# The first expert pair of each pass moved from steps 1 to 3 to steps 3 to 5, with four kept output tiles

## The chip, the core and the metric

The kernel runs on one core of a Trainium2 chip. The core has four compute engines that work side by side: TensorE (PE in the rows), VectorE (DVE), ScalarE (ACT) and GpSimd (POOL). SyncE (SP) issues DMAs and computes nothing here; POOL issues the indirect ones. The metric is the device time of one execution in microseconds. Three timed runs of the kernel before gave 3048.73, 3056.23 and 3058.16 us; the median is 3056.23 us.

## The reference, cut to what matters

32 images of 32 x 32 tokens with 128 channels pass through three layers, each added to its input:

```
x = x + shifted_window_attention(groupnorm(x))     # 8 heads of 16, windows of 64 tokens, scaled cosine
t = t + banded_attention(layernorm(t))             # 4 heads of 32, windows of 128, the last 33 keys
t = t + experts(layernorm(t))                      # below
probs = softmax(xf @ gate_w + gate_b)
top2_vals, top2_idx = top_k(probs, 2)              # each token goes to 2 of 8 experts
h = gelu(xf @ w1[e] + b1[e])                       # 128 -> 256
y = h @ w2[e] + b2[e]                              # 256 -> 128
out = sum over the two experts of share * y
```

The reference computes every expert for every token. The kernel computes only the two chosen ones: tokens are scattered to a buffer in DRAM that is sorted by expert, and read back in tiles of 512 slots that belong to one expert each.

## The kernel before, in words

The program is a pipeline over images. A pass `i` (-1 to 34) works on image `i` in the first attention, on `i - 1` and `i - 2` in the second, on `i - 3` in the gate, and on expert tiles of image `i - 4` or older. Each pass has 8 steps `t` of one kind: every engine walks through the same list of steps, and semaphores keep them together. A step holds the softmax of one 128-token tile of either attention (names that end in `_a` and `_b`) and some pieces of the other stages. The order on each engine is written out by hand and no scheduler changes it.

The chain of one step is: PE makes scores (L625, L635) in `bank_s`; DVE adds the bias (L1500, L1503) and takes row maxima (L1508); POOL subtracts the maxima (L1133); ACT takes the exponential (L984); PE transposes (L686); ACT copies (L979); PE multiplies by the values in the next step (L695 to L708). The start of L1500 is the start of a step in what follows.

The expert work is 135 tiles of 512 slots. One image's scattered tokens are a batch: four tiles, made into two pairs (the first batch has one tile, the last one 18). A pass has two slots, 0 and 1, for one pair each. A pair goes through three stages in three steps:

- `into`: PE transposes the tokens of the pair into `bank_m` (`slots_in`, L743) and ACT copies them to `xe` (L1005) and the rows' numbers to `back_to` (L1008).
- `mid`: PE multiplies by the first weights (`hidden`, L752), ACT applies gelu (L1015). ACT loads the table of gelu ahead of it (L1109) and the table of exp behind it (L1036).
- `back`: PE multiplies by the second weights (`expert_out`, L759), DVE adds the bias (L1485) and multiplies by the share into `yo` (L1491).

Slot 0 has its stages in steps 1, 2, 3; slot 1 in steps 6, 7 and step 0 of the next pass. Both use the one PSUM pair `bank_m`, one after the other. SP loads each tile's tokens and weights (`load_pair`, L457 and L459) into one of 4 buffers. POOL adds `yo` to the output in DRAM with an indirect accumulating DMA of 128 rows (`add_back`, L1157), four to a tile; the first of the four waits until the tile before has landed. `BACK_AT` says in which step, counted from the pair's own pass, each of a pair's eight add-backs stands: 8 is step 0 of the next pass. POOL also scatters a new image's tokens, 16 indirect DMAs a pass (L1140), four each in steps 5, 6, 7 and 0.

`plan()` deals pairs to slots: slot 0 takes a pair from pass `batch + 5` on, slot 1 from pass `batch + 4` on. What is left after pass 33 is the tail: pairs that run one after the other in four sets of PSUM banks, with nothing beside them but the add-backs.

## Time and profile before

| what | value |
|---|---|
| median of 3 runs | 3056.23 us |
| the profiled execution: its own time | 3051.38 us |
| the profiled execution: span | 3049.6 us |
| mean granted TensorE clock | 0.891 |
| PE, DVE, ACT, POOL busy | 79%, 66%, 59%, 62% of the span |
| PE in slices 2 to 34 of 40 | 0.8 or 0.9 busy |
| POOL at the end | alone; it ends the span |

The trace covers one execution. Its span is 1.8 us shorter than the time of that execution, and that time is 4.85 us under the median. The busy shares are means over three different stretches: filling (to about pass 6), the full pipeline (passes 7 to 31), and the tail. No engine is full in any of them by its mean; the length is set step by step.

### The profile page before, as it was taken

How to read it: one execution, taken by the hardware profiler on the slowest of the kernel's cores; microseconds unless marked ns; L12 is line 12 of the kernel's file. 1: busy time of each engine (PE TensorE's matmuls, PEld its weight loads, DVE VectorE, ACT ScalarE, POOL GpSimd, SP SyncE). 2: the span in 40 equal slices, each digit the busy share in tenths (PEclk: the TensorE clock that was granted, in tenths of full speed). 3: DMA queues.
4: the chain of work that ended last, by engine and by line, in shares of the span. 5: the costliest groups of instructions: out<-in, count | busy, mean ns of one | idle time of the engine just before them, and what ended most of it. 6: DMA issues, size and time to landing. Idle time of an engine off the chain costs nothing. (4 is left out here: it accounts for less than half of the span.)

```text
span 3049.6 us, 72894 instructions
## 1 busy us (share of the span) xinstructions
PE 2417.9 (79%) x26418; PEld 1716.6 (56%) x26418; DVE 1998.0 (66%) x5670; ACT 1786.3 (59%) x3430; POOL 1897.7 (62%) x1569
## 2 busy tenths in 40 slices
PE   6898888888888888888888888888888888765650
PEld 3465556566556666565556666565566666553440
DVE  3588876777677777776776776777776777662110
ACT  3666666666666666666666666666666666542220
POOL 0224455766666666766666667766666667776666
PEclk8999989999999999989999999999999999877775
DMA  2011122333333333323333333333333323335442
GB/s 77 16 34 37 48 71 55 81 67 70 71 74 74 77 76 63 81 62 74 70 74 74 77 65 76 80 63 75 70 74 74 77 56 71 82 62 141 89 82 26
DMA packets 247793, 210.77 MB, mean 69 GB/s; under 512 B 35260, under 2 KB 204360, under 8 KB 247248
## 3 DMA queue, kind: packets, MB, share of 16 engines
q0 software_dynamic: 94144, 69.54, 16.1%
q1 hardware_dynamic: 153296, 136.58, 15.9%
q8 instruction: 215, 3.52, 0.5%
q14 instruction: 138, 1.13, 0.1%
HBM read 119.73 MB, written 90.77 MB: 69 GB/s over the span
## 5 line engine op out<-in xcount | busy, mean ns | idle before, releaser
L1157 POOL DMA_INDIRECT out_dram<-yo,back_to x540 | 855.3, 1584 | 228.2 <-issue 174.4
L1133 POOL TENSOR_TENSOR s_sb_a<-s_sb_a,mx_a 128x512 f32<-128x512 f32 x256 | 282.4, 1103 | 771.1 <-DVE mx_a L1508 770.8
L1140 POOL DMA_INDIRECT x_sorted<-xn_c,place_i x512 | 515.3, 1006 | 138.9 <-issue 133.4
L1500 DVE TENSOR_TENSOR s_sb_a<-bank_s,bias_a 128x512 f32<-128x512 f32 x256 | 176.0, 687 | 308.4 <-PE bank_s L625 251.4
L1133 POOL TENSOR_TENSOR s_sb_b<-s_sb_b,mx_b 128x512 f32<-128x512 f32 x256 | 289.2, 1130 | 6.9 <-DVE mx_b L1508 6.9
L759 PE MATMUL bank_m<-wk_e,hid 128*128 128x128 f32 x1840 | 282.0, 327 | 0.9 <-ACT hid L1015 0.9
L759 PEld LDWEIGHTS bank_m<-wk_e,hid 128*128 128x128 f32 x1840 | 279.9, 244 | 1.7 <-issue 1.7
L752 PE MATMUL bank_m<-xe,wk_e 128*128 128x512 f32 x460 | 231.4, 628 | 34.4 <-ACT hid L1015 25.8
L686 PE MATMUL bank_to<-k_consts,p_sb_b 128*128 128x128 f32 x1024 | 182.7, 305 | 88.1 <-ACT pt_sb_a L979 76.7
L984 ACT ACTIVATE p_sb_a<-s_sb_a 128x512 f32<-128x512 f32 x256 | 160.5, 627 | 149.8 <-POOL s_sb_a L1133 149.8
L979 ACT ACTIVATE pt_sb_b<-bank_to 128x512 f32<-128x512 f32 x256 | 152.6, 596 | 155.4 <-PE bank_to L686 154.8
L625 PE MATMUL bank_s<-kk_a,q_a 32*64 32x128 f32 x4096 | 123.3, 295 | 129.0 <-ACT sq_a L949 43.2
L1015 ACT ACTIVATE hid<-bank_m,wk_e 128x512 f32<-128x512 f32 x230 | 154.0, 686 | 66.8 <-PE bank_m L752 60.3
L686 PEld LDWEIGHTS bank_to<-k_consts,p_sb_b 128*128 128x128 f32 x1024 | 116.4, 150 | 134.3 <-ACT pt_sb_a L979 118.8
L686 PE MATMUL bank_to<-k_consts,p_sb_a 128*128 128x128 f32 x1024 | 169.3, 289 | 26.2 <-ACT p_sb_a L984 22.0
L984 ACT ACTIVATE p_sb_b<-s_sb_b 128x512 f32<-128x512 f32 x256 | 161.4, 630 | 44.4 <-POOL s_sb_b L1133 42.2
L1485 DVE TENSOR_TENSOR bank_m<-bank_m,wk_e 128x512 f32<-128x512 f32 x115 | 80.2, 699 | 149.5 <-PE bank_m L759 149.5
L1503 DVE TENSOR_TENSOR s_sb_b<-bank_s,k_consts 128x512 f32<-128x512 f32 x256 | 174.2, 680 | 5.5 <-PE bank_s L635 5.5
L1508 DVE TENSOR_REDUCE mx_a<-s_sb_a 128x8 f32<-128x512 f32 x256 | 173.0, 676 | 0.4
L1508 DVE TENSOR_REDUCE mx_b<-s_sb_b 128x4 f32<-128x512 f32 x256 | 173.0, 676 | 0.4
L996 ACT ACTIVATE sum_inv<-bank_to 128x256 f32<-128x256 f32 (+1 forms) x268 | 99.9, 373 | 124.0 <-PE bank_to L708 104.8
L625 PEld LDWEIGHTS bank_s<-kk_a,q_a 32*64 32x64 f32 x4096 | 65.1, 131 | 178.9 <-issue 177.3
(230 smaller groups left out, 5761.9 us busy)
## 6 DMA issues: line engine op xcount, KB each, us to landing
wk_e<-in_w_experts_dram SPq DMA_DIRECT2D x127, 321.0 KB, 3.3
xs<-x_sorted SPq DMA_DIRECT2D x127, 260.0 KB, 2.8
xin<-in_x_dram SPq DMA_DIRECT2D x128, 112.0 KB
x_res<-in_x_dram SPq DMA_DIRECT2D x256, 56.0 KB
out_dram<-t SPq DMA_DIRECT2D x256, 56.0 KB
out_dram<-yo,back_to POOLq DMA_INDIRECT x540, 3.4
x_sorted<-xn_c,place_i POOLq DMA_INDIRECT x512
x_res<-in_x_dram SPq DMA_DIRECT2D x256, 8.0 KB
```

Source lines behind the costliest of these rows:

```text
L625: last = mm(S[r][WTOK * j:WTOK * j + WTOK, 0:P].rearrange("p (h n) -> p h n", h=2), q_flat[rows, window(2 * ta + j)], keys[rows, :, window ...
L686: last = tr(T[:, P * j:P * j + P], p_sb[w][:, j, :], ident)
L752: mm(banks[:, ch, :], w[:, P * ch:P * ch + P], xe[:, m, :], start=True, stop=True).then_inc(z_ready, 1)
L759: last = mm(banks[:, m, P * j:P * j + P], hid[:, CH * m + ch, P * j:P * j + P], w[:, HID + P * ch:HID + P * ch + P], start=(ch == 0), stop ...
L984: func(flat(p_sb[w][:, :, :]), flat(s_sb[w][:, :, :]), ACT.Exp, scale=1.0 if w == 0 else float(DB) ** -0.5).then_inc(p_ready[w], 1)
L1015: func(hid[:, CH * m + ch, :], banks[:, ch, :], ACT.Gelu, bias=w[:, B1_AT + ch:B1_AT + ch + 1]).then_inc(gelu_ready, 1)
L1133: pool.tensor_tensor(s[:, :, :], s[:, :, :], m[:, :, None].to_broadcast(shape), ALU.subtract).then_inc(s_sub[w], 1)
L1140: pool.indirect_dma_start(out=x_sorted.ap(), out_offset=bass.IndirectOffsetOnAxis(ap=place_i[:, d % 2, TILES * choice + t:TILES * choice + ...
L1157: pool.indirect_dma_start(out=out, out_offset=bass.IndirectOffsetOnAxis(ap=back_to[:, q % IDS, j:j + 1], axis=0), in_=yo[:, q % YO, j, :], ...
L1500: tt(s_sb[0][:, :, :].rearrange("p (r h) n -> p r (h n)", h=2), scores, bias_a[:, kind, :, :].rearrange("p (r h) n -> p r (h n)", h=2), AL ...
L1503: tt(s_sb[1][:, :, :], scores, const("mask_b")[:, None, :].to_broadcast([P, HB, P]), ALU.add).then_inc(s_added[1], 1)
L1508: dve.tensor_reduce(mx_s[w][:], s_sb[w][:, :, :], AX_X, ALU.max).then_inc(s_max[w], 1)
```

## The change

Slot 0 moves from steps 1, 2, 3 to steps 3, 4, 5. It now takes a pair from pass `batch + 4` on, as slot 1 does, so that both slots of a pass work on the two pairs of one batch. SP loads both pairs together, where it loaded slot 1's alone; the load of the next pass's slot 0, later in the pass, is gone. `yo` holds 4 tiles in place of 3. The add-backs of slot 0 stand in steps 6, 7, 8, 9 (one each) and 10 (four), those of slot 1 in 11 and 12 (four each).

```diff
-IDS, YO = 8, 3
+IDS, YO = 8, 4
-BACK_AT = ((4, 4, 4, 4, 5, 6, 7, 8), (9, 9, 9, 9, 10, 10, 10, 10))
+BACK_AT = ((6, 7, 8, 9, 10, 10, 10, 10), (11, 11, 11, 11, 12, 12, 12, 12))
@@ plan()
-            if i >= pairs[u].batch + (5 if n == 0 else 4) and i < PASSES - FREE_PASSES:
+            if i >= pairs[u].batch + 4 and i < PASSES - FREE_PASSES:
@@ stage()
-            into = slot(i, 0) if t == 1 else slot(i, 1) if t == 6 else None
-            mid = slot(i, 0) if t == 2 else slot(i, 1) if t == 7 else None
-            back = slot(i, 0) if t == 3 else slot(i - 1, 1) if t == 0 else None
+            into = slot(i, 0) if t == 3 else slot(i, 1) if t == 6 else None
+            mid = slot(i, 0) if t == 4 else slot(i, 1) if t == 7 else None
+            back = slot(i, 0) if t == 5 else slot(i - 1, 1) if t == 0 else None
@@ sync
-                if here[1] is not None:
-                    load_pair(sp, here[1])
+                for u in here:
+                    if u is not None:
+                        load_pair(sp, u)
                 if on(a):
                     load_residual(a, 0)
-                following = slots[i + 1][0] if i + 1 < PASSES else None
-                if following is not None:
-                    load_pair(sp, following)
@@ tensor, step
-                if t == 1:
+                if t == 3:
                     read_slots()
@@ scalar, step
-                if t == 1 and into is not None:
+                if t == 3 and into is not None:
                     slots_copy(into, bank_m)
```

On PE, from the score matmuls of step 4 (L625) to the first matmul of the gate's places and the q and k projections, the kernel before has:

```order
L759 MATMUL bank_m<-wk_e,hid 128x128 x16
L658 MATMUL bank_s<-wqkv_s,xt_b 128x128 x4
...
L686 MATMUL bank_to<-k_consts,p_sb_a 128x128 x4
L625 MATMUL bank_s<-kk_a,q_a 64x128 x8
L635 MATMUL bank_s<-k_b,q_b 128x128 x4
L686 MATMUL bank_to<-k_consts,p_sb_b 128x128 x4
L670 MATMUL bank_to<-chosen,earlier 128x72
```

The same place of the changed kernel, whose lines are two lower (L757 is `expert_out`, L750 `hidden`, L741 `slots_in`):

```order
L741 MATMUL bank_m<-k_consts,xs 128x128 x8
L684 MATMUL bank_to<-k_consts,p_sb_a 128x128 x4
L623 MATMUL bank_s<-kk_a,q_a 64x128 x8
L633 MATMUL bank_s<-k_b,q_b 128x128 x4
L684 MATMUL bank_to<-k_consts,p_sb_b 128x128 x4
L750 MATMUL bank_m<-xe,wk_e 128x512 x4
L668 MATMUL bank_to<-chosen,earlier 128x72
```

The 16 matmuls of `expert_out` have left step 3, the transposes of `slots_in` have come to its end, and the 4 of `hidden` stand between the transposes of step 4 and the matmul L670 (now L668).

On POOL, from the subtraction of step 1 to the one of step 5, the kernel before has (L1133 is the subtraction, L1157 the add-back, L1140 the scatter):

```order
L1133 TENSOR_TENSOR s_sb_b<-s_sb_b,mx_b 128x512
L1157 DMA out_0_dram<-yo,back_to 33280x128 x4
L1133 TENSOR_TENSOR s_sb_a<-s_sb_a,mx_a 128x512
L1133 TENSOR_TENSOR s_sb_b<-s_sb_b,mx_b 128x512
L1157 DMA out_0_dram<-yo,back_to 33280x128 x4
L1133 TENSOR_TENSOR s_sb_a<-s_sb_a,mx_a 128x512
L1133 TENSOR_TENSOR s_sb_b<-s_sb_b,mx_b 128x512
L1133 TENSOR_TENSOR s_sb_a<-s_sb_a,mx_a 128x512
L1133 TENSOR_TENSOR s_sb_b<-s_sb_b,mx_b 128x512
L1157 DMA out_0_dram<-yo,back_to 33280x128 x4
```

The changed kernel (L1131 the subtraction, L1155 the add-back):

```order
L1131 TENSOR_TENSOR s_sb_b<-s_sb_b,mx_b 128x512
L1155 DMA out_0_dram<-yo,back_to 33280x128
L1131 TENSOR_TENSOR s_sb_a<-s_sb_a,mx_a 128x512
L1131 TENSOR_TENSOR s_sb_b<-s_sb_b,mx_b 128x512
L1155 DMA out_0_dram<-yo,back_to 33280x128 x4
L1131 TENSOR_TENSOR s_sb_a<-s_sb_a,mx_a 128x512
L1131 TENSOR_TENSOR s_sb_b<-s_sb_b,mx_b 128x512
L1155 DMA out_0_dram<-yo,back_to 33280x128 x4
L1131 TENSOR_TENSOR s_sb_a<-s_sb_a,mx_a 128x512
L1131 TENSOR_TENSOR s_sb_b<-s_sb_b,mx_b 128x512
L1155 DMA out_0_dram<-yo,back_to 33280x128 x4
```

Before, steps 1, 2 and 4 have four add-backs and step 3 none. Now step 1 has one, and steps 2, 3 and 4 have four each. At the end of POOL's program the tail has 88 add-backs in place of 96.

## Rows read from the trace of the kernel before

**Rows 1.** Busy time by stretch: start:end, length, engines (instructions), TensorE clock, DMA share, GB/s

```profile
413.00:488.10 75.10, 62.77 (x753) 44.69 (x753) 56.63 (x170) 49.38 (x98) 40.05 (x37) 0.89 0.28 74
488.10:576.60 88.50, 75.05 (x817) 53.86 (x817) 61.80 (x177) 55.75 (x107) 56.08 (x47) 0.88 0.31 69
576.60:2549.70 1973.10, 1656.19 (x18791) 1192.78 (x18791) 1417.25 (x4049) 1277.73 (x2439) 1330.50 (x1105) 0.92 0.34 72
2549.70:2810.00 260.30, 184.58 (x1649) 135.07 (x1649) 148.02 (x434) 115.31 (x225) 187.34 (x155) 0.82 0.40 86
2810.00:3049.60 239.60, 97.55 (x464) 73.90 (x464) 26.75 (x41) 36.46 (x63) 149.24 (x96) 0.69 0.43 72
```

**Rows 2.** The same view, pass 19: its steps 0 to 7 in order

```profile
1522.08:1532.24 10.16, 8.94 (x124) 8.03 (x124) 8.55 (x24) 5.53 (x12) 8.41 (x8) 1.00 0.41 102
1532.24:1542.77 10.53, 9.45 (x113) 7.87 (x114) 8.17 (x29) 4.02 (x10) 8.25 (x7) 0.84 0.40 57
1542.77:1554.76 11.99, 9.42 (x90) 5.04 (x89) 6.06 (x18) 10.87 (x23) 9.18 (x7) 0.98 0.61 127
1554.76:1568.52 13.76, 12.09 (x128) 11.24 (x129) 9.59 (x20) 5.00 (x12) 2.03 (x2) 0.77 0.06 10
1568.52:1579.56 11.04, 8.20 (x90) 4.24 (x88) 8.17 (x41) 5.29 (x9) 8.02 (x6) 0.85 0.59 146
1579.56:1588.70 9.14, 6.81 (x81) 3.64 (x81) 4.82 (x11) 8.24 (x13) 6.33 (x7) 1.00 0.16 29
1588.70:1596.39 7.69, 6.54 (x101) 5.51 (x101) 7.61 (x21) 6.55 (x14) 6.56 (x6) 1.00 0.25 48
1596.39:1607.45 11.06, 10.11 (x97) 6.00 (x97) 8.03 (x16) 10.03 (x20) 9.06 (x10) 1.00 0.28 60
```

**Rows 3.** The same view, pass 6: its steps 1 to 3

```profile
422.97:432.58 9.61, 8.49 (x104) 6.91 (x105) 8.17 (x28) 3.62 (x9) 6.84 (x5) 0.82 0.30 50
432.62:439.41 6.79, 5.42 (x82) 3.51 (x80) 6.65 (x18) 5.25 (x15) 3.59 (x3) 1.00 0.81 203
439.41:447.35 7.94, 6.13 (x96) 5.07 (x97) 7.80 (x17) 4.89 (x11) 2.49 (x2) 1.00 0.04 12
```

**Rows 4.** Order of time, PE: start, duration, instruction, count, idle time before and its releaser

```profile
1546.18 1.96 PE L752 MATMUL bank_m<-xe,wk_e 128*128 128x512 f32 x4 [0.79 <-ACT hid L1015]
1556.34 5.98 PE L759 MATMUL bank_m<-wk_e,hid 128*128 128x128 f32 x32
...
1571.64 0.22 PE L670 MATMUL bank_to<-chosen,earlier 128*128 128x72 bf16 x1 [2.78 <-DVE ot_b L1524]
1571.97 3.31 PE L726 MATMUL bank_s<-xn_a,wq_s 128*128 128x512 f32 x4
1575.12 1.88 PE L726 MATMUL bank_s<-xn_a,wk_s 128*128 128x512 f32 x4
...
1587.67 0.48 PE L625 MATMUL bank_s<-kk_a,q_a 32*64 32x128 f32 x16 [1.44 <-ACT sq_a L949]
...
1589.16 1.04 PE L743 MATMUL bank_m<-k_consts,xs 128*128 128x128 f32 x8
...
2698.86 3.74 PE L759 MATMUL bank_m<-wk_e,hid 128*128 128x128 f32 x32
```

**Rows 5.** Order of time, POOL, pass 19 and the tail

```profile
1530.11 0.97 POOL L1140 DMA_INDIRECT x_sorted<-xn_c,place_i  x1 [0.30 <-issue]
...
1538.34 1.57 POOL L1157 DMA_INDIRECT out_dram<-yo,back_to  x1 [0.30 <-issue]
...
3007.36 1.55 POOL L1157 DMA_INDIRECT out_dram<-yo,back_to  x1 [2.46 <-DVE yo L1491]
```

**Rows 6.** Order of time, ACT, the stage mid of pass 19

```profile
1547.37 1.49 ACT L1015 ACTIVATE hid<-bank_m,wk_e 128x512 f32<-128x512 f32 x2 [0.76 <-PE bank_m L752]
1548.88 1.28 ACT L1036 ACT_TABLE_LOAD   x1
```

**Rows 7.** DMA issues on SP, slot 1's first tile of pass 19

```profile
1543.69 0.38 SPq L457 DMA_DIRECT2D xs<-x_sorted  x1
```

## The prediction

> **What bounds the kernel now.** I read the busy time by long stretches first. Passes 8 to 30 are 23 passes in 1973.10 us, 85.8 us each, so that stretch is 65% of the span; pass 6, in which only slot 1 is filled, took 75.10 and pass 7, the first with both, 88.50. Passes 31 to 34 take 260.3 us up to the tail, and the tail 239.6 [rows 1]. The reader is to see that a change to a pass counts some 24 times, and one to the tail once.
>
> Then the same view by steps, pass 19 [rows 2]. No engine fills its step. The longest steps are those of slot 0: step 2 (11.99 us, ACT busy 10.87) and step 3 (13.76 us, PE busy 12.09, TensorE clock 0.77 of full, POOL busy 2.03). Steps 5 and 6 have no second or third stage of a pair and take 9.14 and 7.69. In pass 6, which has slot 1 but not slot 0, steps 1 to 3 take 9.61, 6.79 and 7.94, and there DVE is the full engine (6.65 of 6.79, 7.80 of 7.94) [rows 3]. So slot 0 costs 0.92 + 5.20 + 5.82 = 11.9 us where it stands now. Third, the timeline of PE: in step 3 the 32 matmul records of `expert_out` take 5.98 us at the low clock, 3.74 at the full one; in step 4 PE stands idle 2.78 us until DVE has written `ot_b`, and the q projection behind takes 3.31 where the like k projection takes 1.88; in step 5 it waits 1.44 for ACT's `sq_a` [rows 4]. Those idle times are where the three stages go.
>
> **The change, part by part.** I take a pass as pass 19 and work out its steps anew.
>
> Steps 1 and 2 lose slot 0. I give them pass 6's 9.61 and 6.79 [rows 3].
>
> Step 3 gains the transposes of `into`, 1.04 us on PE [rows 4], between the value products and the transposes of the probabilities. Step 3 is then DVE's, 7.94 us, and DVE gets nothing. The delay reaches the next step's scores by a few tenths: 8.3.
>
> Step 4 gains `hidden` of two tiles, 1.96 + 0.79 + 1.96 = 4.7 us with the wait for gelu between [rows 4]. It stands ahead of L670, which waits 2.78 us anyhow, so 1.9 show. PE is busy in that gap, and the q projection may run at the full clock, 1.88 for 3.31: -1.4. ACT gets two table loads of 1.28 us [rows 6] and four gelus; it is busy 5.29 of 11.04 [rows 2], and its `xe` copy at the end of step 3 decides when `hidden` starts. That start depends on POOL, below. Without it: 11.04 + 1.9 - 1.4 = 11.5, and 0.2 to 0.4 for the copy, 11.8. If the clock falls all the same, 13.2.
>
> Step 5 gains `expert_out`, 3.74 us at the full clock [rows 4]. It stands ahead of the norms' matmuls, whose results ACT waits for. PE has 9.14 - 6.81 = 2.3 us free [rows 2], of which 1.44 is the wait for ACT that would have ended anyhow. I take 2.0 to show: 11.1. Bounds: 1.4 (all free time used) and 3.7 (none). DVE's four operations here find it 4.82 of 9.14 busy.
>
> Steps 6, 7 and 0 stay: 7.69, 11.06, 10.16 [rows 2]. Sum so far: 10.16 + 9.61 + 6.79 + 8.3 + 11.8 + 11.1 + 7.69 + 11.06 = 76.5 us.
>
> POOL then has to be laid over this. An add-back is 1.57 + 0.30 = 1.87 us, a scatter 1.27, the two subtractions of a step 2.03 and some 0.16 [rows 2, 5]. A pass has 16 of each DMA and eight pairs of subtractions: 29.9 + 20.3 + 17.5 = 68 us. That fits in 76.5, but not step by step: with four add-backs steps 2, 3 and 4 need 9.7 us each, 29.0 in all, against 6.8 + 8.3 + 11.8 = 26.9. POOL may start 1.9 us into step 2 (L1500 to the maxima), is free 11.5 us in, and the maxima of step 3 are there at 8.7: 2.8 late. In step 4 it is some 4.2 late, by step 5 about 2. The late subtraction of step 3 delays both exponentials, ACT's copies behind them, and so `xe` and `hidden`. Before, POOL was late by about as much in step 7 with no harm visible, so part is slack: I take 1.6 us of the 2.8, with 0 and 4.2 as ends. A pass is 76.5 + 1.6 = 78.1 us.
>
> Here a rule speaks against the change. Beside the add-backs now put in step 3, DVE runs operations with two SBUF inputs. The trace's nearest rows are the add-backs of pass 19, 1.57 us beside any DVE work [rows 5]. The Trainium skill, SBUF — State Buffer, in the part on the "DVE blocks DMA" trap, says that GpSimd writes the descriptors of its DMAs through a port pair that DVE can hold, and waits meanwhile. By the row the add-backs cost nothing more; by the rule the sum would be up to one DVE operation higher in each pass.
>
> Loads: slot 1's first load goes out at 1543.69, 0.9 us into step 2 [rows 7]; now slot 0's goes there and slot 1's behind it. The data is wanted at the end of step 3, 13 us on. I cost it at nothing; if the DMA engines were full (share 0.81 in step 2 of pass 6 [rows 3]) add-backs would land later, and the first of each four would wait. The end of a tile costs 2.46 us when nothing hides it [rows 5]; in a pass two subtractions hide most of it. This is in the bound of 4.2 above.
>
> `YO` = 4: slot 0's outputs in step 5 need the room of the pair one pass older, which is added back by step 2. No wait, no gain.
>
> Outside the full passes: pass 7 falls from 88.5 to 78.1, -10.4. Pass 6 now has slot 0 in steps 3 to 5, but no third stage in step 0: I leave it at 75.1. Passes 31 to 34: POOL is busy 187 us of 260 and with issue gaps near full [rows 1]; five more add-backs (9.4 us) wait for it at the start of pass 31, and it gets back the idle time of two step 3s. I take 0, between -15 and +15. Tail: one pair was moved forward to pass 6, so 22 tiles remain in place of 24. A tile is four add-backs of 1.55, three gaps of 0.3 and one of 2.46 for the landing, 9.6 us [rows 5]; two make -19.2. The last image's first pair is now the third of the tail and not the fourth; its tokens can be loaded only when they are scattered, and two pairs of add-backs (38 us) still lie between.
>
> Sum: 23 x (85.8 - 78.1) = 177; with 10.4 and 19.2, -207. On the profiled execution's 3051.4 us this is 2845; the median lies 4.85 higher: 2850 us.
>
> **The rivals.**
>
> A, the clock and POOL take more. The clock falls in step 4 as before (+1.4), and POOL's lateness counts in full (+2.6): a pass of 82.1, 24 of them +96, 2946 us. For it: `hidden` has a 0.8 us gap for gelu in it and a late start, and in pass 19 the clock fell behind such gaps (0.77 in step 3 [rows 2]). Against it: PE is denser in steps 4 and 5.
>
> B, the idle time swallows nearly all. PE needs 1.04 + 3.8 + 3.74 = 8.6 us for the pair and had 2.8 + 2.3 + 1.8 us idle in steps 4, 5 and 3. With POOL harmless and the clock higher in step 1 too, a pass is 75.3: 24 x -2.8 = -67, 2783 us. Against: ACT's chain in step 5.
>
> C, slower: POOL becomes serial with the softmax in steps 2, 3 and 4. If the landing is not hidden, each takes 9.7 + 2.5 = 12.2, and if the next scores wait for it, 1.9 more: 42.3 us in place of 26.9. The pass is then 76.5 + 15.4 = 91.9, and the kernel 2850 + 24 x 13.8 = 3181 us. It decides from 7.7 us more in a pass than in the forecast: there the pass is back at 85.8. For it: three steps in a row with four add-backs, where before no more than two stood together. Against: in the two (steps 1 and 2) POOL was busy 8.25 of 10.53 and 9.18 of 11.99 [rows 2], and all steps ahead and behind leave it room.
>
> D, no change: the stages only trade places, as when ACT bounds all (10.87 of 11.99 in step 2) and step 4 grows by step 2's 5.2 and step 5 by step 3's 5.8. That is 10.16 + 9.61 + 6.79 + 8.3 + 16.2 + 14.9 + 7.69 + 11.06 = 84.7 a pass, 3056 - 23 x 1.1 - 3.8 - 19.2 = 3008 us, still faster; if passes 31 to 34 and POOL's lateness take 39 us more, it is no change.
>
> **How the numbers follow.** The forecast, 2800 to 2900 us, has 0.62; A 0.22; B 0.08; C 0.04; D 0.04. The predicted time is the forecast's, 2850. The range reaches down to 2785, B's value, and up to A's, 2946. A change under 0.3% (9 us) can't be told from none here. Faster: forecast, A, B and half of D, 0.94; same 0.02; slower: C, 0.04.
>
> **What would show it.** In the changed profile a pass is 76 to 80 us (DVE's first operation of step 0 to the next); step 2 is 6.8 to 7.5 with DVE over 0.9 busy; step 3 under 9.5; step 5 about 11; PE's wait ahead of the places' matmul is under 0.5; the tail has 88 add-backs, still 9.65 us a tile. POOL's idle time ahead of the `s_sb_a` subtraction is near zero in steps 3 and 4. It is wrong if step 4 is over 14.5 us, if the subtractions are what the exponentials wait for in steps 3 and 4 by more than 3 us, or if PE waits for a tile's load in step 3.

## The result, and the profile after

The changed kernel takes 2881.52 us (median of four runs, 2872.67 to 2882.43), against 3054.06 us for the kernel before beside it: a ratio of 0.943, 95% interval 0.9405 to 0.9454. The forecast was 2850, the range 2785 to 2946. The profiled execution took 2882.43 us. This is the head of its page, which answers to the table of the profile before:

```profile
span 2880.6 us, 72895 instructions
PE 2340.9 (81%) x26418; PEld 1648.3 (57%) x26418; DVE 2088.5 (73%) x5670; ACT 1782.6 (62%) x3432; POOL 1906.8 (66%) x1569
```

The work is the same and the span is 169.0 us shorter. PE is busy 77 us less (2417.9 before) with the same 26418 matmul records, which goes with the granted clock (0.921 on average for 0.891); DVE is busy 90 us more (1998.0 before) with the same 5670 instructions, which nothing in the change asks for. The mean clock of the stretches is the number ahead of the DMA share in the rows below. Busy time by stretch, the cuts where those of [rows 1] are (pass 6, pass 7, passes 8 to 30, passes 31 to 34, tail):

```profile
408.58:482.49 73.91, 65.37 (x785) 46.34 (x785) 62.45 (x173) 55.06 (x105) 41.13 (x39) 0.95 0.28 75
482.49:559.79 77.30, 67.56 (x817) 48.38 (x817) 64.47 (x177) 55.24 (x107) 58.17 (x49) 0.98 0.38 80
559.79:2386.50 1826.71, 1591.91 (x18791) 1139.01 (x18791) 1493.33 (x4049) 1273.35 (x2439) 1339.81 (x1105) 0.96 0.37 78
2386.50:2657.30 270.80, 179.32 (x1601) 130.55 (x1601) 151.32 (x431) 110.88 (x218) 195.52 (x160) 0.79 0.40 84
2657.30:2880.60 223.30, 96.92 (x464) 67.57 (x464) 26.05 (x40) 35.60 (x63) 136.81 (x88) 0.71 0.44 74
```

Everything up to pass 8 is 16.8 us shorter (559.8 for 576.6; 11.2 of it in pass 7), passes 8 to 30 are 146.4 us shorter, passes 31 to 34 are 10.5 us longer, and the tail is 16.3 us shorter. That adds up to 169.0. Of the 16.8, the 4.4 that lie before pass 6 are scatter: in the traces of the runs below pass 6 begins anywhere from 406.7 to 422.6 us, with no edit that bears on it. So the gain is where the forecast had it, in the passes, but a pass lost 6.4 us and not 7.7. The steps of pass 19, which answer to [rows 2]:

```profile
1436.64:1446.80 10.16, 8.94 (x124) 8.03 (x124) 8.57 (x25) 5.53 (x12) 8.40 (x8) 1.00 0.40 100
1446.80:1457.60 10.80, 10.02 (x104) 8.61 (x104) 8.24 (x30) 3.57 (x9) 4.42 (x4) 0.68 0.28 43
1457.60:1464.39 6.79, 5.56 (x82) 3.66 (x82) 6.65 (x17) 5.25 (x15) 4.35 (x4) 1.00 0.58 170
1464.39:1473.42 9.03, 7.06 (x102) 5.69 (x103) 8.89 (x17) 4.97 (x12) 7.00 (x6) 1.00 0.77 183
1473.42:1486.07 12.65, 11.33 (x102) 5.81 (x103) 9.31 (x41) 11.60 (x18) 10.83 (x8) 1.00 0.36 43
1486.07:1496.89 10.82, 9.62 (x110) 6.66 (x108) 6.65 (x16) 7.72 (x13) 9.11 (x8) 1.00 0.27 38
1496.89:1504.59 7.70, 6.53 (x101) 5.51 (x101) 7.62 (x22) 6.56 (x14) 4.97 (x5) 1.00 0.15 41
1504.59:1515.65 11.06, 10.11 (x97) 6.00 (x97) 8.71 (x16) 10.03 (x20) 9.05 (x10) 1.00 0.27 61
```

Step 2 is pass 6's step to the hundredth (6.79, DVE 6.65 busy). Steps 3 and 4, where the clock stood at 0.77 and 0.85, now have it at 1.00; step 1 has it at 0.68. Step 4 is the longest, with PE and ACT both over 11.3 us busy in it.

One pass is one sample, so the table below has means over passes 8 to 30 (from DVE's first operation of a step to that of the next). It carries the rest of this text. The column "us" is the median of the timed runs, the others are from the one profiled execution.

| kernel | 0 | 1 | 2 | 3 | 4 | 5 | 6 | 7 | pass | us |
|---|---|---|---|---|---|---|---|---|---|---|
| before | 10.35 | 10.45 | 11.97 | 13.65 | 11.24 | 9.14 | 7.69 | 11.29 | 85.79 | 3054 |
| forecast | 10.16 | 9.61 | 6.79 | 8.3 | 11.8 (+1.6) | 11.1 | 7.69 | 11.06 | 78.1 | 2850 |
| after | 10.30 | 10.07 | 6.80 | 9.07 | 12.87 | 11.06 | 7.76 | 11.48 | 79.42 | 2881.5 |
| e1, a quarter of the add-backs | 10.57 | 9.38 | 6.79 | 7.96 | 11.44 | 10.53 | 7.69 | 11.44 | 75.81 | 2741.8 |
| e2, add-backs spread | 10.79 | 9.96 | 7.02 | 8.14 | 11.26 | 10.53 | 7.69 | 11.09 | 76.48 | 2806.6 |
| e3, second load later | 10.65 | 9.67 | 6.80 | 9.16 | 12.06 | 11.86 | 7.85 | 11.34 | 79.40 | 2884.0 |
| e4, old dealing | 10.28 | 9.93 | 6.80 | 9.06 | 13.06 | 10.94 | 7.71 | 11.32 | 79.10 | 2892.8 |
| e5, add-backs alone | 10.28 | 10.41 | 11.93 | 13.47 | 11.55 | 9.14 | 7.69 | 11.22 | 85.70 | 3060.7 |
| e6, residual first | 10.30 | 9.75 | 6.80 | 8.44 | 13.57 | 11.05 | 7.84 | 11.37 | 79.11 | 2871.9 |
| e7, e2 with a filler matmul | 10.64 | 9.17 | 7.33 | 8.44 | 11.39 | 10.54 | 7.69 | 11.09 | 76.29 | 2806.0 |
| e8, `hidden` behind the places | 10.23 | 9.57 | 6.80 | 9.05 | 15.50 | 10.54 | 7.69 | 11.76 | 81.14 | 2923.1 |
| e9, two-input compares | 10.72 | 9.66 | 6.80 | 9.11 | 12.92 | 11.13 | 7.87 | 11.35 | 79.56 | 2884.0 |
| e10, early weights | 10.29 | 9.67 | 6.80 | 9.07 | 12.56 | 11.55 | 7.72 | 11.24 | 78.91 | 2884.5 |
| e11, early weights on e2 | 10.65 | 9.99 | 6.97 | 8.30 | 11.34 | 10.53 | 7.69 | 11.09 | 76.55 | 2814.1 |

**PE, where the stages went.** In order of time, start, duration, idle time before; steps 3 to 5 of pass 19, the lines that answer to [rows 4]:

```profile
1469.44 1.09 PE L741 MATMUL bank_m<-k_consts,xs 128*128 128x128 f32 x8
...
1474.21 1.98 PE L750 MATMUL bank_m<-xe,wk_e 128*128 128x512 f32 x4 [0.26 <-ACT xe L1003]
1476.98 1.96 PE L750 MATMUL bank_m<-xe,wk_e 128*128 128x512 f32 x4 [0.79 <-ACT hid L1013]
1478.78 0.20 PE L668 MATMUL bank_to<-chosen,earlier 128*128 128x72 bf16 x1
1478.81 0.35 PE L670 MATMUL bank_to<-chosen,ones 128*128 128x64 bf16 x8
1479.02 1.96 PE L724 MATMUL bank_s<-xn_a,wq_s 128*128 128x512 f32 x4
...
1485.97 3.74 PE L757 MATMUL bank_m<-wk_e,hid 128*128 128x128 f32 x32
```

The places' matmul (L668) stood behind 2.78 us of idle time and now has none, in any of passes 8 to 30; the q projection takes 1.96 where it took 3.31; `expert_out` takes 3.74 where it took 5.98.

**POOL, where the price is.** The same stretch:

```profile
1467.48 1.81 POOL L1155 DMA_INDIRECT out_dram<-yo,back_to  x1 [0.31 <-DMA out_dram<-yo,back_to]
1468.73 1.63 POOL L1131 TENSOR_TENSOR s_sb_a<-s_sb_a,mx_a 128x512 f32<-128x512 f32 x1
1469.73 1.62 POOL L1131 TENSOR_TENSOR s_sb_b<-s_sb_b,mx_b 128x512 f32<-128x512 f32 x1
1472.77 1.56 POOL L1155 DMA_INDIRECT out_dram<-yo,back_to  x1 [1.41 <-issue]
...
1478.39 1.57 POOL L1155 DMA_INDIRECT out_dram<-yo,back_to  x1 [0.30 <-issue]
1479.39 1.64 POOL L1131 TENSOR_TENSOR s_sb_a<-s_sb_a,mx_a 128x512 f32<-128x512 f32 x1
1480.39 1.63 POOL L1131 TENSOR_TENSOR s_sb_b<-s_sb_b,mx_b 128x512 f32<-128x512 f32 x1
```

No idle time stands before the subtractions. Over passes 8 to 30 the first one starts 2.47 us after its maxima are there in step 3, 4.20 in step 4 and 1.34 in step 5, where on time is 0.09. The forecast had 2.8, 4.2 and 2. These starts are those of the records, and a late subtraction's record begins 0.57 us before the add-back ahead of it ends (1468.73 against 1467.48 + 1.81 = 1469.29); its end comes 1.07 us behind the add-back's. So the 1.63 us of the rows is the usual 1.03 and the rest of the add-back, and not a slower subtraction. The first add-back of step 3 waits 1.41 us for the tile before it to land (1.25 us on average beyond the usual gap of 0.3). What follows on ACT:

```profile
1470.40 0.63 ACT L982 ACTIVATE p_sb_a<-s_sb_a 128x512 f32<-128x512 f32 x1 [2.82 <-POOL s_sb_a L1131]
...
1473.14 1.02 ACT L1003 ACTIVATE xe<-bank_m 128x1024 f32<-128x1024 f32 x1
```

The exponential waits 2.82 us (also the mean of step 3 over passes 8 to 30, where it waited 0.00 before), the `xe` copy stands behind it, and `hidden` starts at 1474.21. And on DVE, first in pass 12, then in pass 19, operations that took 0.2 us each in the kernel before:

```profile
922.02 3.11 DVE L1411 TENSOR_SCALAR cmp_c<-rank_c 128x64 f32<-128x64 f32 x2
...
1469.34 2.08 DVE L1381 TENSOR_SCALAR chosen<-rank_c 128x64 bf16<-128x64 f32 x1
...
1480.54 1.65 DVE L1411 TENSOR_SCALAR cmp_c<-rank_c 128x64 f32<-128x64 f32 x2
```

`chosen` starts at 1469.34, beside the first late subtraction, and ends at 1471.42, where the second ends (1469.73 + 1.62 = 1471.35). `cmp_c` ends at 1482.19; the second subtraction of step 4 ends at 1482.02. In pass 12 `cmp_c` begins 0.9 us before the end of the last add-back (922.91) and is held through it and both subtractions. The kernel before had this wait too, in step 7, where a subtraction is late as well; its pass 18:

```profile
1513.93 1.65 POOL L1133 TENSOR_TENSOR s_sb_a<-s_sb_a,mx_a 128x512 f32<-128x512 f32 x1
1513.95 2.66 DVE L1394 COPY xn_c<-weight 128x4 f32<-128x4 f32 x1
```

The change brought the wait to steps 3 and 4. The groups of `chosen` and `cmp_c<-rank_c`, total and mean ns, in the kernel before (L1383, L1413) and after (L1381, L1411):

```profile
L1413 DVE TENSOR_SCALAR cmp_c<-rank_c 128x64 f32<-128x64 f32 x64 | 8.5, 199 | 0.0
L1383 DVE TENSOR_SCALAR chosen<-rank_c 128x64 bf16<-128x64 f32 x32 | 6.2, 195 | 1.1
```

```profile
L1381 DVE TENSOR_SCALAR chosen<-rank_c 128x64 bf16<-128x64 f32 x32 | 57.4, 1793 | 1.1
L1411 DVE TENSOR_SCALAR cmp_c<-rank_c 128x64 f32<-128x64 f32 x64 | 44.8, 742 | 0.0
```

That is 87.5 us of the 90 by which DVE got busier: time in which it held an instruction and, as far as the rows tell, did nothing: e6 below starts `chosen` later, and it ends with the subtractions all the same.

### The profile page after: what moved, and what is told of

It reads as the page before. It is cut to its first block and busy times, and to the rows that moved or that the text cites. A ratio compares the mean times of both kernels' runs of the same rounds, so it can differ in the third digit from the quotient of the medians.

```text
span 2880.6 us, 72895 instructions
## 1 busy us (share of the span) xinstructions
PE 2340.9 (81%) x26418; PEld 1648.3 (57%) x26418; DVE 2088.5 (73%) x5670; ACT 1782.6 (62%) x3432; POOL 1906.8 (66%) x1569
## 5 line engine op out<-in xcount | busy, mean ns | idle before, releaser
L1155 POOL DMA_INDIRECT out_dram<-yo,back_to x540 | 864.9, 1602 | 271.7 <-issue 209.9
L1131 POOL TENSOR_TENSOR s_sb_a<-s_sb_a,mx_a 128x512 f32<-128x512 f32 x256 | 329.6, 1288 | 547.7 <-DVE mx_a L1506 547.6
L1131 POOL TENSOR_TENSOR s_sb_b<-s_sb_b,mx_b 128x512 f32<-128x512 f32 x256 | 333.9, 1304 | 9.2 <-DVE mx_b L1506 9.2
L982 ACT ACTIVATE p_sb_a<-s_sb_a 128x512 f32<-128x512 f32 x256 | 161.0, 629 | 234.9 <-POOL s_sb_a L1131 234.5
L750 PE MATMUL bank_m<-xe,wk_e 128*128 128x512 f32 x468 | 246.2, 654 | 46.1 <-ACT hid L1013 31.4
L684 PE MATMUL bank_to<-k_consts,p_sb_b 128*128 128x128 f32 x1024 | 175.4, 296 | 97.5 <-ACT pt_sb_a L977 83.2
L757 PE MATMUL bank_m<-wk_e,hid 128*128 128x128 f32 x1872 | 226.8, 281 | 0.9 <-ACT hid L1013 0.9
L757 PEld LDWEIGHTS bank_m<-wk_e,hid 128*128 128x128 f32 x1872 | 222.1, 198 | 2.0 <-issue 1.9
L750 PEld LDWEIGHTS bank_m<-xe,wk_e 128*128 128x128 f32 x468 | 86.9, 206 | 167.0 <-issue 131.8
L684 PEld LDWEIGHTS bank_to<-k_consts,p_sb_a 128*128 128x128 f32 x1024 | 111.7, 145 | 87.8 <-issue 51.3
```

The costliest lines, as they stand in the source:

```text
L684: last = tr(T[:, P * j:P * j + P], p_sb[w][:, j, :], ident)
L750: mm(banks[:, ch, :], w[:, P * ch:P * ch + P], xe[:, m, :], start=True, stop=True).then_inc(z_ready, 1)
L757: last = mm(banks[:, m, P * j:P * j + P], hid[:, CH * m + ch, P * j:P * j + P], w[:, HID + P * ch:HID + P * ch + P], start=(ch == 0), stop ...
L982: func(flat(p_sb[w][:, :, :]), flat(s_sb[w][:, :, :]), ACT.Exp, scale=1.0 if w == 0 else float(DB) ** -0.5).then_inc(p_ready[w], 1)
L1131: pool.tensor_tensor(s[:, :, :], s[:, :, :], m[:, :, None].to_broadcast(shape), ALU.subtract).then_inc(s_sub[w], 1)
L1155: pool.indirect_dma_start(out=out, out_offset=bass.IndirectOffsetOnAxis(ap=back_to[:, q % IDS, j:j + 1], axis=0), in_=yo[:, q % YO, j, :], ...
```

## The experiments

**1. How much of a pass is the add-backs?** e1 issues only the first of each four add-backs in the passes, so most of the output is missing; it is a probe and no version of the kernel. (The code cuts in this part show the lines that matter; waits that count add-backs or operations are adapted to them.)

```
-    if when == t + TILES * (i - j):
+    if when == t + TILES * (i - j) and m % SUB == 0:
```

> The changed kernel, but in the passes only the first of a tile's four add-backs is issued (12 of 16 in a pass are left out; the tail keeps all four), so three quarters of most tiles' outputs are not added. Theory, POOL is late: four add-backs in each of steps 2, 3 and 4 make the subtractions of steps 3 and 4 late and put them beside DVE's operations; without them step 3 goes from 9.07 us to 7.95, step 4 from 12.9 to 11.5 or less, a pass from 79.4 to 76.5 to 77, and the kernel from 2881 to about 2815 us (24 passes of 2.5, and some 5 at the end). Rival, PE and ACT bound steps 4 and 5 and the add-backs are hidden: step 3 and 4 stay within 0.3 us, the kernel at 2865 to 2880.

2741.81 us, ratio 0.8995 (0.8974 to 0.9016). With the subtractions on time a pass is 75.81, 3.6 us less than after: steps 3, 4 and 5 are 1.1, 1.4 and 0.5 shorter, a little more than the theory's 76.5 to 77. The total fell by 140 us, more than either expectation: the 23 passes make 83 us of it, and passes 31 to 34 lost another 54.6 us (270.8 to 216.2). Those four hang on POOL, and neither theory had thought of them.

**2. The place of the add-backs in a pass.** e2 has 1, 4, 2, 2, 4, 1, 1 and 1 add-backs in steps 0 to 7, where the changed kernel has 4 in each of steps 2 to 4.

```
-BACK_AT = ((6, 7, 8, 9, 10, 10, 10, 10), (11, 11, 11, 11, 12, 12, 12, 12))
+BACK_AT = ((5, 6, 7, 8, 9, 9, 9, 9), (10, 10, 11, 11, 12, 12, 12, 12))
```

> The changed kernel with all add-backs, placed in other steps: slot 0 in 5, 6, 7, 8 and four in 9, slot 1 in 10, 10, 11, 11 and four in 12, so that by step from 0 to 7 there are 1, 4, 2, 2, 4, 1, 1, 1 in place of 1, 1, 4, 4, 4, 0, 1, 1. Theory, POOL is late: steps 2 and 3 need 5.9 us of POOL and fit, so step 3 falls to 8.0 and step 4 to about 11.8; the pass is 77 to 77.5 and the kernel 2825 to 2835 us. Rival, the number of add-backs counts and not their place: POOL has the same 68 us a pass, and the kernel stays within 0.3% of 2881 us. Second rival, step 1 with four add-backs grows as it was in the kernel before (10.5 for 10.0): then 2840 to 2850.

2806.57 us, ratio 0.9199 (0.9184 to 0.9214): the best version with the whole output, 2.6% under the changed kernel, and below the bands of the theory and of both rivals. The theory's cause held; it had step 4 at 11.8 where it is 11.26. Its steps 2 to 4 of pass 19, and three groups of it:

```profile
1423.89:1431.25 7.36, 5.62 (x82) 3.67 (x82) 7.22 (x17) 5.66 (x15) 5.90 (x6) 1.00 0.74 169
1431.25:1439.38 8.13, 7.17 (x105) 6.00 (x105) 7.99 (x17) 5.62 (x14) 7.23 (x5) 1.00 0.90 213
1439.38:1450.64 11.26, 10.29 (x96) 4.95 (x94) 8.01 (x41) 10.30 (x17) 8.40 (x7) 1.00 0.34 42
```

```profile
L1131 POOL TENSOR_TENSOR s_sb_a<-s_sb_a,mx_a 128x512 f32<-128x512 f32 x256 | 287.5, 1123 | 511.0 <-DVE mx_a L1506 510.7
L982 ACT ACTIVATE p_sb_a<-s_sb_a 128x512 f32<-128x512 f32 x256 | 160.8, 628 | 102.5 <-POOL s_sb_a L1131 102.1
L1381 DVE TENSOR_SCALAR chosen<-rank_c 128x64 bf16<-128x64 f32 x32 | 6.2, 195 | 1.1
```

```profile
L1131 POOL TENSOR_TENSOR s_sb_a<-s_sb_a,mx_a 128x512 f32<-128x512 f32 x256 | 329.6, 1288 | 547.7 <-DVE mx_a L1506 547.6
L982 ACT ACTIVATE p_sb_a<-s_sb_a 128x512 f32<-128x512 f32 x256 | 161.0, 629 | 234.9 <-POOL s_sb_a L1131 234.5
```

The last two rows are the changed kernel's: the exponentials wait 234.9 us for POOL there and 102.5 in e2. The mean of the subtraction's records, 1.29 for 1.12 us, differs only by how many are late and begin inside an add-back. In e2 every subtraction of steps 0 to 6 is on time, `chosen` is back at 195 ns, and a pass is 76.48. The same sixteen add-backs thus cost 2.9 us a pass by their place alone.

**3. The landing.** In the changed kernel four tiles are loaded in step 2, one after the other. e3 issues slot 1's loads behind the residual's.

```
-                for u in here:
-                    if u is not None:
-                        load_pair(sp, u)
+                if here[0] is not None:
+                    load_pair(sp, here[0])
                 if on(a):
                     load_residual(a, 0)
+                if here[1] is not None:
+                    load_pair(sp, here[1])
```

> The changed kernel with slot 1's pair loaded behind load_residual(a, 0), so after step 3, and only slot 0's pair in step 2. In the changed kernel POOL stood 2.9 us idle ahead of the first add-back of step 3, waiting for the landing of the tile before. Theory, the four tile loads side by side make that landing late: the wait falls to 1 us or less, step 4's subtraction comes 2 us sooner, and 1 us of step 4 goes in most passes: 2855 to 2865 us. Rival, the landing takes that long whatever else moves, and the kernel stays within 0.3% of 2881 us.

2883.97 us, ratio 0.9443 (0.9419 to 0.9468), no change from after. The wait ahead of step 3's first add-back fell from 1.25 to 0.44 us, but that of the next four rose from 0.48 to 1.37, and what step 4 gave (0.8) step 5 took. The theory had the cause right for one place and missed that the same transfers meet the next four.

**4. The dealing.** e4 deals slot 0 as the kernel before did, one pass later.

```
-            if i >= pairs[u].batch + 4 and i < PASSES - FREE_PASSES:
+            if i >= pairs[u].batch + (5 if n == 0 else 4) and i < PASSES - FREE_PASSES:
```

> The changed kernel with the old rule for slot 0 (a pair from pass batch + 5 on); stages, add-backs and loads as changed. Theory, the gain is in the passes and the dealing only moves one pair out of the tail: the tail has 24 tiles again and takes 19 us more (9.8 each), pass 6 loses its first slot and 4 us; the kernel is 2893 to 2900 us, passes 79.4 as in the changed kernel. Rival, that both pairs of one batch stand in one pass matters to the passes themselves (landing, waits for scatters): then passes change by over 0.5 us and the kernel leaves 2885 to 2905 us.

2892.8 us, ratio 0.9483 (0.9457 to 0.9509), at the lower edge of what the theory had (2893 to 2900): passes at 79.10, and the tail back at 238.2 us with 24 tiles. Passes 31 to 34 stay at 270.6, so their extra 10.5 us aren't the dealing's.

**5. The add-backs alone.** e5 is the kernel before, with the changed kernel's `BACK_AT` and `YO` = 4.

```
-IDS, YO = 8, 3
+IDS, YO = 8, 4
-BACK_AT = ((4, 4, 4, 4, 5, 6, 7, 8), (9, 9, 9, 9, 10, 10, 10, 10))
+BACK_AT = ((6, 7, 8, 9, 10, 10, 10, 10), (11, 11, 11, 11, 12, 12, 12, 12))
```

> The kernel before, with only the new places of the add-backs and four kept tiles; stages, dealing and loads as before. Theory, the gain comes from the stages' places and the add-backs' new places alone cost: POOL is late by 2.5 us in step 3 as in the changed kernel, but step 3 is 13.8 us long and takes it; passes 85.5 to 87, the kernel 3050 to 3085 us. Rival, four kept tiles and spread add-backs carry part of the gain: then under 3035 us.

3060.72 us, ratio 1.0019 (1.0006 to 1.0032). The passes are unchanged (85.70), and against what I wrote no subtraction is late: with step 2 at 11.9 us four add-backs fit into it. So the same twelve add-backs in a row are harmless in long steps and cost 2.9 us in short ones. Passes 31 to 34 took 274.4 us, 14 more than before, with the stages and the dealing as before. That leaves the place of the add-backs and the fourth kept tile; e2, with four kept tiles and other places, has 263.6 there, so most of it is the place.

**6. DVE's order in step 3.** `chosen` meets POOL's late subtraction, and the residual, which `xn_a` follows, stands behind it. e6 moves `chosen` behind the residual.

```
                     if on(b):
                         window_residual(b, 0)
+                    if on(d):
+                        gate_chosen(d)
```

> The changed kernel, with one DVE operation of step 3 in another place: chosen<-rank_c (64 elements, 0.2 us before, 2.09 in the changed kernel while POOL subtracts) stands behind the addition t<-bank_s,x_res, which reads PSUM, in place of ahead of it. Theory, DVE is held by the late subtractions and not by its own work: the addition fits in the wait, step 3 falls from 9.07 to 8.5 us and chosen takes 1.5 us in place of 2.09; step 4 may give part back. The kernel 2866 to 2876 us. Rival, the long duration is not a wait for POOL's subtractions but the operation's own: it stays 2.09 us and step 3 at 9.07.

2871.9 us, ratio 0.9395 (0.9379 to 0.9411). Step 3 lost 0.6 us and step 4 took 0.7; `chosen` takes 1.60 us (median): it begins 0.5 us later and ends with the second subtraction as before, so its length is a wait and not its own, and the rival falls. The total lies in the expected band, but the pass is only 0.3 shorter, which is no more than its scatter (a standard deviation of 1.1 to 1.3 over 23 passes, some 0.25 for each mean). I count it as unclear.

**7. Clock in step 1.** In e2 it is 0.76 there. e7 is e2 with one more matmul in that step, whose result nothing reads.

```
+                if t == 1 and i >= first_slots and tiled(n) and slots[i][0] is not None:
+                    after(pe, yo_ready, pairs[slots[i][0]].first)
+                    mm(bank_m[:, 0, :], ident, k[:, 0:HALF], start=True, stop=True)
```

> The kernel with spread add-backs (2806.6 us) plus one extra 128x512 matmul with no use in step 1 of each pass, in the place where PE waits 0.6 us for DVE. Theory, the low clock of step 1 (0.76 there) costs 1 to 1.5 us a pass and follows PE's idle time around the start of step 1: with the filler the clock of step 1 is over 0.9 and the kernel is 2775 to 2795 us. Rival, the clock fell for the idle time in step 0, ahead of the filler, and the filler adds 0.9 to 1.9 us to step 1: 2825 to 2850 us.

2805.99 us, ratio 0.9178 (0.9163 to 0.9194): e2's time, between the theory's band and the rival's. The clock of step 1 rose to 0.89 and the step fell from 9.96 to 9.17, but steps 2, 3 and 4 grew by 0.31, 0.30 and 0.13. The clock of step 3 fell from 1.00 to 0.92, which may be a part of it. What step 1 gave, the next three took: most of the 0.8 us was not to be had there.

**8. Does `hidden` lie in idle time?** e8 puts it behind the places' matmuls in step 4.

```
-                if mid is not None: ...
+                if t != 4:
+                    both_hidden()
 ...
                     places(d)
+                if t == 4:
+                    both_hidden()
```

> The changed kernel with hidden of slot 0 put behind the places' matmuls in step 4 in place of ahead of them. Theory, hidden is cheap in step 4 because it fills PE's wait for ot_b: now that wait (2 to 2.8 us) is open again and step 4 grows by 2 to 2.5 us, more if the clock falls in it; the kernel 2930 to 2960 us. Rival, step 4 ends by the late subtraction on POOL and the chain behind it, and PE's place for hidden is of no weight: within 0.4 us of 12.9 in step 4, the kernel 2870 to 2892 us.

2923.11 us, ratio 0.9562 (0.9546 to 0.9578). PE in step 4 of its pass 19:

```profile
1509.41 0.19 PE L668 MATMUL bank_to<-chosen,earlier 128*128 128x72 bf16 x1 [2.75 <-DVE ot_b L1526]
1509.44 0.35 PE L670 MATMUL bank_to<-chosen,ones 128*128 128x64 bf16 x8
1509.65 5.54 PE L750 MATMUL bank_m<-xe,wk_e 128*128 128x512 f32 x8
```

The old idle time is back (2.75 us for 2.78), the eight matmul records of `hidden` take 5.54 us where they took 1.98 and 1.96, the clock of step 4 falls to 0.85 on average, and the step is 2.6 us longer. Steps 1 and 5 gave back 0.5 each, so the total ended just under the expected band. The cover that the forecast named is real.

**9. Which DVE operations wait beside a late subtraction?** Over the 23 passes of the changed kernel step 4 goes with the time of the two `cmp_c` compares: from 11.78 us at 0.88 to 14.31 at 3.39, slope 0.95, correlation 0.96. e9 computes `chosen` and `cmp_c` with two-input operations against a constant; the cut shows `cmp_c`.

```
-  ts(choice[:, n, :, :], rank_c[:, :, :], float(n), None, ALU.is_equal)
+  tt(choice[:, n, :, :], rank_c[:, :, :], const("levels")[:, n:n + 1, None].to_broadcast([P, TILES, E]), ALU.is_equal)
```

> The changed kernel, but `chosen` and the two halves of `choice` are computed by TENSOR_TENSOR against a broadcast constant in place of TENSOR_SCALAR. Question: what stretches DVE's small compares in steps 3 and 4 (`chosen` 2.09 us for 0.19, `cmp_c` up to 3.11 for two, in pass 12 of the changed kernel) when POOL's late subtractions run beside them? Theory: a TENSOR_SCALAR from SBUF to SBUF does not run until both subtractions are through, while a two-input operation shares with them: the worst the trace of the changed kernel shows of one beside a subtraction is 1.41 for 0.69 (`cmp_c<-cmp_c`). Then `chosen` takes 0.2 to 0.9 us, step 3 falls from 9.07 to 7.9 to 8.4 (DVE is busy 8.89 of 9.03 there), step 4 by 0 to 1.5, and the kernel takes 2835 to 2865 us (2881.5 before). Rival 1: any small operation of DVE waits the same beside a subtraction; `chosen` stays near 2.1 and the time within 0.3% of the changed kernel's. Rival 2: the compares get short, but the time does not move, because steps 3 and 4 hang on POOL's lateness alone: `chosen` under 0.9, step 3 at 9.0, 2875 to 2885 us.

2883.96 us, ratio 0.9449 (0.9427 to 0.947); the theory fell, and rival 1 has its numbers. The group in e9:

```profile
L1382 DVE TENSOR_TENSOR chosen<-rank_c,k_consts 128x64 bf16<-128x64 f32 x32 | 58.3, 1822 | 1.1
```

Two inputs wait as one did (1822 for 1793). Rival 1's wording goes too far, though, as it is not every small operation: in the changed kernel the median of `ot_a<-bank_to,sum_inv`, with one input in PSUM, is 0.28 us whether it starts inside a subtraction (138 times) or clear of one (105), and that of `st_b<-t` 0.28 in both; that of `chosen` is 2.09 inside (25 times) and 0.195 clear (5).

**10 and 11. Is it DVE's queue that ends step 4?** Both kernels compute `cmp_c<-rank_c` and `weight` in DVE's idle time ahead of `place` (the semaphore counts shift by four), e10 on the changed kernel, e11 on e2.

```
                 if t == 4 and on(d):
+                    gate_weights(d)
                     gate_places(d)
```

> The changed kernel, but DVE computes `choice` and `weight` (four operations, 0.35 + 0.29 + 0.29 us, `cmp_c<-rank_c` and behind it) in its idle time of step 4 ahead of `place` (2.92 us in pass 19) and no longer behind it. In the changed kernel step 4 is 12.87 us on average and goes with the time of the two compares (11.78 us with 0.88, 14.31 with 3.39; slope 0.95 over 23 passes); the forecast without POOL was 11.8. Theory A: what stands behind `place` on DVE ends step 4, and POOL's two late subtractions hold back whichever operation with SBUF operands meets them: the wait passes on to the next such operation (`cmp_c<-cmp_c,place`), which becomes 1 to 2.5 us long, and only what was taken out of the queue is won: 0.8 to 1.0 us a pass, step 4 at 11.9 to 12.1, 2855 to 2865 us. Theory B: the stretch belongs to the compares; moved, they take 0.35, and step 4 falls to 10.5 to 11.2: 2830 to 2845 us. Rival: step 4 does not hang on DVE's queue but on POOL's lateness through ACT: step 4 stays over 12.5, time within 0.3% of the changed kernel's 2881.5.

> The same edit laid over e2_adds_spread (add-backs 1, 4, 2, 2, 4, 1, 1, 1 by step, subtractions on time; 2806.6 us, step 4 at 11.26). If DVE's queue behind `place` ends step 4 there too, 0.6 to 1.0 us a pass go: step 4 at 10.3 to 10.7, 2783 to 2793 us. Rival: with the subtractions on time PE (`hidden` ahead of the places and the projections behind) or ACT ends step 4, and the time stays at 2800 to 2810 us.

e10 took 2884.54 us, ratio 0.9454 (0.9433 to 0.9476). The wait passed on, as theory A had it: the compares are short (255 ns mean), and the next operation has it,

```profile
L1425 DVE TENSOR_TENSOR cmp_c<-cmp_c,place 128x128 f32<-128x128 f32 x32 | 51.5, 1610 | 0.1
```

and in order of time, the first operation of step 5 of its pass 19:

```profile
1490.74 0.69 DVE L1504 TENSOR_TENSOR s_sb_a<-bank_s,bias_a 128x512 f32<-128x512 f32 x1 [0.59 <-PE bank_s L633]
```

The gain did not come: step 4 at 12.56 and the total are those of e10's rival. DVE's queue is done earlier and then waits 0.59 us for PE's scores: step 4 lost 0.3 us only and step 5 took 0.5. Over passes 8 to 30 DVE's idle time ahead of step 5 is 0.05 us on average in the changed kernel (under 0.05 in 18 of the 23) and 0.49 in e10, in every pass. So the correlation above misled me: DVE's queue ended step 4 in the changed kernel, but PE's scores came only a few tenths sooner. That they are so late because of the late exponentials fits e2, and no run shows it by itself. e11 took 2814.13 us, ratio 0.9206 (0.9191 to 0.9222), a pass of 76.55, no better than e2. Its rival was right in kind, the time 4 us over its band: in e2 DVE already waits 0.67 us for PE's scores ahead of step 5, with ACT busy 10.30 and PE 10.29 of 11.26 in step 4, and in e11 it waits 1.62.

## Why the prediction was right, and what was mis-sized

The direction, the mechanism and the range held; the time came 31 us above the forecast. None of its signs of being wrong came: step 4 is 12.87 us, the exponentials of steps 3 and 4 wait 2.82 and 0.43 us for the subtractions, and PE waits for no load in step 3. By its own steps:

- **Steps 1 and 2 lose slot 0** (9.61, 6.79): 10.07 and 6.80. Right for step 2; step 1 is 0.46 over, and its clock is 0.76 and not pass 6's 0.82.
- **Step 3, 8.3**: 9.07. With the add-backs off or spread it is 7.96 and 8.14, so 8.3 was right for the stage and the rest is POOL's.
- **Step 4, 11.8, with 1.6 for POOL 13.4**: 12.87. 11.44 and 11.26 in e1 and e2. e8 shows the cover, the wait for `ot_b`. The clock held (0.98), which rival A had against it.
- **Step 5, 11.1**: 11.06. Of it 0.5 is POOL's lateness (10.53 in e1 and e2); the stage itself cost 1.4, the lower of the two bounds and not the 2.0 taken.
- **Steps 6, 7 and 0** were to stay: 7.76, 11.48 and 10.30, within 0.2 of the means before. Step 7 is 0.4 over the 11.06 of the sum, which was pass 19's.
- **POOL's lateness**: predicted in place and length (2.8, 4.2, 2; measured 2.47, 4.20, 1.34), and under-priced: 1.6 us a pass, where e2 against after gives 2.9. "Part is slack" was read off step 7 of the kernel before, and two things were wrong in that reading. The subtraction is 1.02 us late there (mean of passes 8 to 30) and not "about as much" as 2.8. And it is not without a trace: ACT's exponential does not wait for it (0.00), but DVE's `xn_c<-weight` is held 2.66 us. In step 3 of the changed kernel the exponential does wait, 2.82 us, ACT's copies and `hidden` queue behind it, and DVE's gate operations stand still. This is the step of the forecast that was mis-sized.
- **The base of the sum**: the steps were taken from pass 19 (85.37 us in all) and held against the mean pass of 85.8, which is 0.4 us more. It did not show in the result, by luck: the sum without POOL was 76.5 and e2 has 76.48, with errors in the steps that cancel (below). So of the 31 us missed in the passes (177 forecast, 146.4 measured) POOL's 1.3 us a pass make 30.
- **The rule on the port pair**: the add-backs take 1602 ns on average against 1584 before, 0.3 us in a pass of sixteen. So the direction that I weighed, DVE holding up the writing of descriptors, is worth 0.3 us at most. The other one is worth more: the Trainium skill, SBUF — State Buffer, in the section "Who interferes with whom", says that an operation of DVE with two SBUF inputs contends with a GpSimd operation that reads SBUF, one in a two-port mode with any GpSimd operation, and that whichever starts first holds the shared port pair for its whole length while the other waits. The trace agrees (2.08 for 0.195 us) and goes further: `chosen` waits through two subtractions and not one. Whether `chosen`, with its one input, ran in a two-port mode no row shows; e9, with two inputs, waited as long. I had looked at the DMAs and not at the subtractions, though the trace of before has the case: `cmp_c<-t,rs_b` takes 1.03 us for 0.34 in the 58 cases in which it begins inside a subtraction.
- **Loads**, taken at nothing: the first add-back of step 3 waits 1.25 us longer for the landing ahead of it. That was foreseen as a part of the lateness and lay within its bounds, and e3 moved the wait without moving the time.
- **Pass 7**, -10.4: -11.2. **Pass 6**, 0: -1.2. The 4.4 us before it are the scatter named above, and luck for the forecast.
- **Passes 31 to 34**, 0 between -15 and +15: +10.5. The term named for it, five add-backs of 1.87 us that wait at the start of pass 31, is 9.4 us, and POOL is busy 8.2 us more there (195.52 for 187.34); the idle time meant to pay for it did not shrink (75.3 us for 73.0). e4 (+10.3), e5 (+14) and e2 (+3.3) put it on the add-backs' place, and e1 (-44) shows that this stretch hangs on POOL.
- **Tail**, -19.2: -16.3, 22 tiles. From one tile's first add-back to the next's it is 10.0 us on average (9.8 before), more than the 9.6 that the forecast added up from single rows; the wait for the landing is 2.9 us on average (2.7 before), as in this row, where the forecast's had 2.46:

```profile
2857.85 1.55 POOL L1155 DMA_INDIRECT out_dram<-yo,back_to  x1 [2.68 <-issue]
```

The tail of the other runs with 22 tiles lies between 218.5 and 223.2 us, so the 2.9 us missed are within its scatter.

Of the rivals, B's sum of idle times comes close for a pass free of POOL's lateness (75.3; e1 has 75.81 and e2 76.48). A's price for POOL, 4.2 us, is 1.3 too high where the forecast's 1.6 is 1.3 too low, and its fall of the clock did not come. C is refuted: POOL did not stay serial with the softmax; it is on time again in step 6. D is refuted by step 4 (12.87 and not 16.2).

What stays open: how the 2.9 us divide between ACT's chain and DVE's blocked operations. e6 and e10 each removed a part of the second and neither moved the time by more than its scatter, so at least one other engine is nearly as late; by DVE's idle time ahead of step 5 in e10 (0.49 us) it is PE. That e2 meets 76.5, the sum worked out without POOL, is partly luck: its steps 4 and 5 are 1.1 us under the forecast's, its steps 0 and 1 1.0 over it, by the clock.

## What to carry to other kernels

When stages leave a step, look at who was hidden by its length: four add-backs fitted into 12 us and did not fit into 6.8, and moving them was worth another 2.6%. Price a late instruction by how late it is and by whether the engine behind it has other work meanwhile, not by a place where it was less late and its reader was busy, and take the steps of a sum and the total it is held against from the same sample. A correlation over passes shows which operation is long when a step is long, not that the step hangs on it; only taking the operation out of the queue tells.

## What the runs showed of the hardware

- Two back-to-back subtractions on GpSimd (128x512 f32, SBUF, 1.03 us each) hold up a small SBUF operation of VectorE until both are through: 2.09 us for 0.195 (`chosen`, 25 cases inside, 5 clear of them). One that begins in the last 1 us of the add-back ahead of a late subtraction is held from there: 2.10 us in the two cases of `chosen` that begin 0.4 us before the subtraction's record, 3.11 for `cmp_c`, at most 3.37 for one (e10). One or two inputs make no difference (e9). Reductions (0.675 us), statistics (0.28) and operations with a PSUM input (0.28) take the same beside a subtraction. The subtractions do not get longer by it: late ones end 1.07 us behind the add-back ahead, although their records show 1.64 us.
- The wait sticks to a place in time and not to an instruction: moved away, it falls on the next such operation (`cmp_c<-cmp_c,place`, 0.26 us clear of a subtraction and 1.89 inside one, e10).
- An idle gap of 2.75 us on PE ahead of 5.5 us of matmuls went with a granted clock of 0.85 over the step; without the gap it was 0.98 (e8 against after).
